# The products that count the experts' choices, issued behind the shared expert's second unit in place of its first

## The reference

```python
h2 = rmsnorm(X, norm2_w).reshape(B * S, d)
logits = h2 @ router_w                      # 8 experts
probs = softmax(logits)
topw, topi = top_k(probs, 2)                # two experts per token
topw = softmax(topw)
shared = swiglu(h2, sh_gate, sh_up, sh_down)   # silu(x @ gate) * (x @ up) @ down, inner width 512
spec = sum over the two chosen experts of topw * swiglu_e(h2)
out = layernorm(x + X + shared + spec)
```

## Time and profile before

| what | value |
|---|---|
| median of 3 runs | 1143.32 us (1141.04 to 1143.38) |
| span of the profiled execution, first to last instruction | 1158.0 us |
| PE busy | 1061.8 us (92%) |
| DVE busy | 802.3 us (69%) |
| ACT busy | 639.9 us (55%) |
| POOL busy | 419.6 us (36%) |

### The profile page before, as it was taken

One profiled execution on the slowest core, in us unless ns is written; L12 is line 12 of the kernel. 1 busy time (PEld: TensorE's weight loads), 2 busy tenths in 40 slices (PEclk: granted clock), 3 DMA queues, 4 the chain that ended last, 5 costly groups with the idle time before them and its releaser, 6 DMA issues. The chain is left out here.

```text
span 1158.0 us, 32282 instructions
## 1 busy us (share of the span) xinstructions
PE 1061.8 (92%) x12782; PEld 994.9 (86%) x12782; DVE 802.3 (69%) x1387; ACT 639.9 (55%) x1337; POOL 419.6 (36%) x483
## 2 busy tenths in 40 slices
PE   3789999999999999999866979899999999999981
PEld 2678889989898999899765978899999999999981
DVE  1668778877778777788646622477788878878544
ACT  1244556555555556566534222367777777877525
POOL 4153334344343344434201476403332323222324
PEclk9999999999999999999987988899999999999995
DMA  7585444444554443440215422347988888776197
GB/s 208 98 189 108 92 99 106 116 112 92 130 111 93 109 104 63 93 75 30 93 38 167 164 96 88 127 138 229 312 260 266 272 283 274 248 270 219 39 211 219
DMA packets 288022, 174.90 MB, mean 151 GB/s; under 512 B 220001, under 2 KB 254433, under 8 KB 286657
## 3 DMA queue, kind: packets, MB, share of 16 engines
q1 hardware_dynamic: 276640, 141.05, 44.5%
q0 software_dynamic: 9648, 29.30, 9.4%
q10 hardware_dynamic: 1584, 2.49, 0.6%
HBM read 129.87 MB, written 52.30 MB: 157 GB/s over the span
## 5 line engine op out<-in xcount | busy, mean ns | idle before, releaser
L1775 POOL DMA_INDIRECT results_scratch<-kept_late,slot_meta x71 | 87.1, 1227 | 255.5 <-ACT kept_late L1385 244.7
L1620 DVE TENSOR_TENSOR prod<-kept_weights,up 128x512 f32<-128x512 f32 (+1 forms) x112 | 71.7, 641 | 76.7 <-ACT kept_weights L1360 25.3
L684 ACT ACTIVATE p3t<-psum 128x512 f32<-128x512 f32 x128 | 68.8, 595 | 89.4 <-PE psum L533 89.4
L1367 ACT ACTIVATE act_hi<-prod 128x512 fp32r<-128x512 f32 x94 | 59.3, 631 | 61.8 <-DVE prod L1620 49.9
L1360 ACT ACTIVATE kept_weights<-gate 128x512 f32<-128x512 f32 (+1 forms) x112 | 62.5, 558 | 54.2 <-PE gate L1267 29.6
L1343 ACT ACTIVATE we_hi<-w_raw 128x1024 fp32r<-128x1024 f32 x81 | 85.7, 1058 | 5.7 <-PE down L1289 5.7
L855 DVE TENSOR_REDUCE max<-psum 128x16 f32<-128x2048 f32 x32 | 73.3, 2292 | 18.2 <-PE psum L519 18.2
L374 PE MATMUL psum<-kept_room,x_hi 128*128 128x512 f32 (+1 forms) x256 | 62.8, 369 | 19.0 <-POOL x_lo L931 19.0
L1629 DVE TENSOR_TENSOR act_lo<-prod,act_hi 128x512 fp32r<-128x512 f32 x94 | 64.5, 686 | 11.9 <-ACT act_hi L1367 9.8
L935 POOL TENSOR_TENSOR ctx_lo<-ctx_t,ctx_hi 128x512 fp32r<-128x512 f32 x16 | 20.6, 1287 | 139.3 <-ACT ctx_hi L594 139.3
L1351 ACT ACTIVATE tok_hi<-turned,norm 128x256 fp32r<-128x256 f32 (+1 forms) x112 | 45.1, 455 | 41.9 <-PE turned L1244 27.4
(11 more groups left out here) (314 smaller groups left out, 3406.1 us busy)
## 6 DMA issues: line engine op xcount, KB each, us to landing
w_raw<-in_w_gate SPq DMA_DIRECT2D x27, 512.0 KB
w_raw<-in_w_up SPq DMA_DIRECT2D x27, 512.0 KB
w_raw<-in_w_down SPq DMA_DIRECT2D x27, 512.0 KB
slots_scratch<-in_empty SPq DMA_DIRECT2D x35, 258.0 KB, 3.3
kept_weights<-slots_scratch SPq DMA_DIRECT2D x31, 258.0 KB
raw_gate<-in_w_gate SPq DMA_DIRECT2D x13, 512.0 KB
h_rows<-in_w_up SPq DMA_DIRECT2D x13, 512.0 KB
h_rows<-in_w_down SPq DMA_DIRECT2D x13, 512.0 KB
```

What stands on the lines that cost most here:

```text
L684: act.activation(p3t[:, a, 4 * j:4 * j + 4, :], bank[f"s3t_{a}"][:, 512 * j:512 * (j + 1)].rearrange("p (h n) -> p h n", h=4), ACT.Exp)\
L1367: act.activation(act_hi[:, n % 2, h * FH:(h + 1) * FH, :], prod[:, h, :].rearrange("p (f n) -> p f n", f=FH), ACT.Copy).then_inc(act_hi_do ...
L1620: dve.tensor_tensor(used(prod[:, h, :], n), used(silu[:, h, :], n), used(up[h][:, :], n), ALU.mult).then_inc(prod_done, 1)
L1775: pool.indirect_dma_start(out=scratch["results"], out_offset=bass.IndirectOffsetOnAxis(ap=slot_meta[:, i % METAS, j, 0:1].bitcast(I32), ax ...
```

## The change

Two lines. On PE the wait for `chosen` and the two counting products move from behind unit 0 to behind unit 1, that is from ahead of `gate_up(1, 0)` to behind `down_unit(0)`. On DVE `count_tiles` moves from half (0, 1) to (1, 1), `find_slots` from (1, 0) to (2, 0), and `place` from (1, 1) to (2, 1). The same instructions are executed; ACT, POOL and SP have the same streams.

```diff
@@ PE, for n in range(UNITS)
                         if is_half(n):
                             turn_products(n)
-                    if n == 0:
+                    if n == 1:
                         pe.wait_ge(loaded, 16 * 3)
                         pe.wait_ge(ones_b_set, 1)
                         pe.wait_ge(chosen_done, 1)
@@ DVE
-                ROUTING = {(0, 0): (choose_second,), (0, 1): (weigh, count_tiles), (1, 0): (find_slots,), (1, 1): (place,)}
+                ROUTING = {(0, 0): (choose_second,), (0, 1): (weigh,), (1, 1): (count_tiles,), (2, 0): (find_slots,), (2, 1): (place,)}
```

## The result

The changed kernel takes 1145.87 us (median of 6 runs, 1144.91 to 1148.29), the kernel before beside it 1141.85 (6 runs, 1140.54 to 1143.38). The ratio is 1.004, with a 95% interval from 1.0027 to 1.0053: slower by 3 to 6 us. The forecast was +3.4 us.

A forecast was written before the change was run, and what follows sets the result against it. PE was taken to bound the kernel through its first tile's turn. Slack falling 9.1 from 3.7 makes PE wait 5.4 us; less 3.6 gained, plus 1.6 low clock, +3.4 on 1143.3: 1146.7 us, 8-in-10 range 1139.0 to 1150.0.

The forecast's parts named there:

- the slack: At the first tile: rows arrive before PE asks for them, by 3.7 us (1.6 to 5.9) in an undisturbed run.
- PE at unit 1: Shared expert's unit 1: the 3.05 us wait goes, with low clock 4.7 us removed; 0.3 to 0.4 us wait added.
- The count and the slots: DVE's routing steps: count starts 5.0 us later, find_slots ends 5.5 us later, and the whole scatter slips by that.
- PE at unit 3: Second half of unit 3: PE waits 1.5 us for DVE's product, yet is 3.6 us ahead of before.
- The low clock behind the wait: After PE's new wait at the first tile: lower clock costs 1.6 us more, bounds 0 to 1.6.
- rival C: At the first tile: rows already last, no slack, whole 5.5 us slip counts, low clock paid in both; 1148.8 us, chance 0.20.
- B's sum: The forecast itself, at the first tile: 5.4 us wait less 3.6 gained plus 1.6 low clock, +3.4 us; chance 0.38.
- The reading of the 14.7 us: Scatter stage: profiled span's 14.7 us excess over the median is profiler disturbance there; unprofiled runs lose about 12 us, not 26.8.
- Rival C's source: Around the kernel: 9 to 15 us of start and end work, so 24 to 30 us missing from the runs' span.
- Rival D: Scatter stage: PE's stalls fall elsewhere, 5.4 us per cluster; one more gives 1145.1, one less 1134.3; chance 0.14.

The follow-up runs named there:

- calm level: Sets of runs in which the unchanged kernel before takes 1141 to 1142 us, with no stalls in the traces.
- padded pair: Kernel before and changed kernel, each with gate and up products of units 5 to 8 made twice (23 us more PE work): 1154.45 and 1151.4 us.
- stalling sets: Sets of runs in which the unchanged kernel before takes 1157 to 1158 us, with stalls in the traces.
- stalling level: The level of 1157 to 1158 us for the unchanged kernel before, with stalls in the traces.
- thirteen units: Kernel before with thirteen shared-expert units ahead of the tiles instead of twelve: 1164.21 us; with counting products behind unit 1's first half and slots found early too: 1164.12.

## Why the prediction was right, and where it wasn't

The direction and the size were right, 1146.7 against 1145.87. That the size came out is partly luck, as one term of the sum, the slack, was wrong in sign. The steps in the order of the prediction:

- **PE at unit 1.** Predicted: no wait ahead of the counting products, full clock, 0.3 to 0.4 us for the product. Measured: none, and 0.28 us. The counting products took 0.67 us (from 637.78 to the next half at 638.45) in place of 1.3.
- **The count and the slots.** Predicted 5.0 later for the count, 5.5 for the scatter. From the start of the mixture the count starts at 24.0 in place of 19.0, and POOL at 37.3 in place of 31.7 in the profile that I had: 5.6. Against the kernel before at the calm level it is 6.1.
- **PE at unit 3.** Predicted a wait of 1.5 and a lead of 3.6; measured 1.47 and, from the start of the mixture, 41.3 - 37.8 = 3.5 against the profile that I had, 2.9 against the kernel before at the calm level (40.8).
- **The slack.** This is the term that I mis-sized. I took 3.7 us for an undisturbed run. At the calm level, where the result was measured, there is none: PE waited 7.4 us for the rows before the change. The faulty step was to set the 14.7 us between the span and the median equal to what PE loses in the scatter. PE comes to the first tile not 14.7 but 146.5 - 118.9 = 27.6 us sooner without the stalls, which is about the whole loss of 26.8 that I had read, and not a part of it. From the start of the mixture to the end the calm trace is only 17.7 us shorter, because 7.4 of the 27.6 us are waited away at the rows and 2.5 go to the lower clock behind that wait. The rows' slip therefore counts whole: the first tile is turned at 132.0 in place of 126.3, 5.7 us later, and no part of PE's 3.5 goes through. The low clock behind the wait, which I added with 1.6, is there in both and cancels (399.7 us from the turn to the end after, 399.6 before). By steps it is rival C, 5.5 us, that happened (5.8 between the two calm traces, from the start of the mixture to the end; 4.0 between the medians), and B's sum came near it (3.4) since its two errors, a slack that isn't there and a clock that is paid anyway, go against each other. The measured 3 to 6 us can't tell the two sums apart; the waits and the padded pair can.
- **The reading of the 14.7 us.** I held them to lie in the scatter stage, and they do: the calm traces have none of the stalls. But I put them down to the profiler, and that fell: in both stalling sets all 11 timed runs of the kernel before lie at 1154 to 1162 us, not a profiled one alone. The first profile has the span and the stalls of that level, and the runs shown beside it have the other. Right place, wrong cause; with the right cause I would have had to ask for both levels, and at both the change loses.
- **Rival C's source.** I quoted the Trainium skill, "Runtime: NRT & Kernel Launch", section "The ~15µs preamble/postamble breakdown", for 9 to 15 us around the kernel. Here the measured time holds 1.8 us around the span (1148.29 and 1146.5), and 2.5 at most in any other run. The microseconds that the page states are thus not in this time, and C came true without them.
- **Rival D** is nearest to what the stalling level shows: there the stalls grew by 6.6 us, near its 5.4 for one cluster. One trace on each side doesn't show that this is its mechanism.

## What to carry to other kernels

A wait that stands alone on the busiest engine is not a gain until it is known which chain arrives last where the next stage begins: here VectorE's small steps release 90 us of scatters, and each microsecond of them counted more than PE's. Filling PE's wait without delaying the other chain gave 0 to 2.5 us; shortening that chain as well, even where PE waits 7 us for it, gave 5 us at the calm level, and nothing that was seen at the stalling level with thirteen units. Before a slack is read from a profile, compare its span with the level of the runs; where they differ by more than the runs among themselves, profile again and look whether the slack is still there.

## What the runs showed of the hardware that I had not expected

- The same kernel has two levels 15 us apart (1141 and 1157), which changed between sets of runs and never among the timed runs of one, and the difference stands in one stage: while POOL issues 64 indirect DMAs, PE loses 27 to 34 us at one level, in stalls that ACT and DVE share (ACT 16.47 us without a named releaser, DVE 5.59 us), and nothing at the other. From the first tile's turn to the end it takes 397 to 398 us at both, where PE didn't wait for the rows.
- A wait of 7.4 us costs PE 1.6 to 2.3 us more behind it at the lower clock; for the removed one of 3.05 us I estimated 1.6 from the earlier trace rows. A wait twice as long costs hardly more: 399.7 us from the turn to the end behind 16.02 us, 400.4 behind 15.83, against 399.6.
- At the stalling level 17.3 us more of PE's work cost 9.3 us in the median, and brought the first tile only 5.4 us later in the trace: added work partly takes the place of stalls.
